# A mixture-of-experts stage that gathers its rows by a map of places instead of scattering them

## What is computed

```
gate_logits = jnp.einsum('bsd,de->bse', x, Wg)
topw, sel = jax.lax.top_k(gate_logits, K)                       # K = 3 of E = 12
topw = jax.nn.softmax(topw.astype(jnp.float32), axis=-1).astype(x.dtype)
cw = jnp.einsum('bsk,bske->bse', topw, jax.nn.one_hot(sel, E, dtype=x.dtype))
h = jax.nn.gelu(jnp.einsum('bsd,edh->ebsh', x, Wup) + bup[:, None, None, :], approximate=False)
y = jnp.einsum('ebsh,ehd->ebsd', h, Wdown) + bdown[:, None, None, :]
return jnp.einsum('bse,ebsd->bsd', cw, y)
...
x = x + jnp.tanh(g_ffn[1]) * _L1_ffn_ref(_layernorm(x, axis=-1), L1_ffn_Wg, ...)
```

## Time and profile before

| | us |
|---|---|
| runs of the kernel, median of 3 | 1554.07 |
| the three runs | 1558.92, 1545.75, 1554.07 |
| the profiled execution | 1544.64 |
| its span, first to last instruction | 1542.9 |

### The profile page before, as it was taken

How to read it: one execution, slowest core, us unless ns; L and a number is a source line. 1 busy time by engine, 2 the same in 40 slices (tenths; PEclk the granted TensorE clock), 3 DMA queues, 4 the chain that set the end, 5 groups by cost and what they waited for, 6 DMA issues and landing times. The chain is left out here.

```text
span 1542.9 us, 35004 instructions
## 1 busy us (share of the span) xinstructions
PE 1288.3 (83%) x13602; PEld 1014.9 (66%) x13602; DVE 1185.3 (77%) x2169; ACT 832.8 (54%) x1807; POOL 252.3 (16%) x213
## 2 busy tenths in 40 slices
PE   3399999668898898898957999984229999999997
PEld 2266776446676676676744676753119998989896
DVE  2656777579999999999753777767319999999995
ACT  1256676335565565565533767641117666667673
POOL 2000000000000000000000000001733454545443
PEclk7558788689999999999786999985559999999999
DMA  7000000032524523523410006200647787888771
GB/s 216 11 5 8 5 5 1 1 81 66 138 61 107 135 64 94 142 71 94 118 56 15 6 9 192 68 1 24 254 142 240 227 245 227 250 225 248 224 217 28
DMA packets 196938, 166.70 MB, mean 108 GB/s; under 512 B 72317, under 2 KB 179985, under 8 KB 196801
## 3 DMA queue, kind: packets, MB, share of 16 engines
q1 hardware_dynamic: 177856, 146.67, 31.8%
q0 software_dynamic: 12880, 13.72, 4.1%
q10 hardware_dynamic: 6064, 4.46, 1.0%
HBM read 116.78 MB, written 50.91 MB: 109 GB/s over the span
## 5 line engine op out<-in xcount | busy, mean ns | idle before, releaser
L1782 POOL DMA_INDIRECT out<-m_yo,m_meta x70 | 170.6, 2437 | 229.2 <-DVE m_yo L1900 200.0
L1804 ACT ACTIVATE m_hf<-m_ps,m_bue 128x256 f32<-128x256 f32 x280 | 117.3, 471 | 118.7 <-PE m_ps L84 117.3
L1051 ACT ACTIVATE f_pr<-f_ps,f_nb 128x256 f32<-128x256 f32 x256 | 107.4, 473 | 104.4 <-DVE f_nb L1314 98.9
L82 PE MATMUL m_ps<-m_xt,m_us 128*128 128x256 f16 x560 | 153.2, 274 | 0.0
L83 PE MATMUL m_ps<-m_xt,m_us 128*128 128x256 f16 x560 | 153.1, 273 | 0.0
L84 PE MATMUL m_ps<-m_xt,m_us 128*128 128x256 f16 x560 | 153.1, 273 | 0.0
L82 PE MATMUL m_ps<-m_ds,m_hs 128*128 128x256 f16 x560 | 152.6, 273 | 0.3 <-DVE m_yo L1900 0.3
L83 PE MATMUL m_ps<-m_ds,m_hs 128*128 128x256 f16 x560 | 152.6, 273 | 0.0
L84 PE MATMUL m_ps<-m_ds,m_hs 128*128 128x256 f16 x560 | 152.6, 273 | 0.0
L472 ACT ACTIVATE x_pr<-x_ps,x_mx 128x120 f32<-128x120 f32 x512 | 143.2, 375 | 7.8 <-DVE x_mx L686 7.8
L690 DVE SCALAR_TENSOR_TENSOR x_pt<-x_ps,x_pt 120x512 f16<-120x512 f32 x128 | 88.3, 690 | 73.2 <-ACT x_pt L480 72.5
(11 more groups left out here) (350 smaller groups left out, 3795.5 us busy)
## 6 DMA issues: line engine op xcount, KB each, us to landing
m_uraw<-in_L_ffn_Wup SPq DMA_DIRECT2D x35, 1024.0 KB
m_draw<-in_L_ffn_Wdown SPq DMA_DIRECT2D x35, 1024.0 KB
expert_in<-x_zeros SPq DMA_DIRECT2D x1, 9520.0 KB, 31.2
m_xg<-expert_in SPq DMA_DIRECT2D x35, 256.0 KB, 4.3
head_values<-f_v_row SPq DMA_DIRECT2D x16, 520.0 KB, 5.2
f_vh<-head_values SPq DMA_DIRECT2D x16, 520.0 KB, 3.6
head_outputs<-f_at_row SPq DMA_DIRECT2D x16, 512.0 KB, 2.9
f_at_in_t<-head_outputs SPq DMA_DIRECT2D x16, 512.0 KB, 6.0
```

Source lines behind the costliest of these rows:

```text
L82: pe.matmul(out, lhs[0], rhs[0], start=(n == 0), stop=False)
L1051: ins = act.activation(pr[h % 2][:, ti, :], S(h)[:, ti, :], ACT.Exp, bias=nb[h % 2][:, ti:ti + 1])
L1782: pool.indirect_dma_start(rows_of, bass.IndirectOffsetOnAxis(meta[j % RING][:, ti, 0:1].bitcast(I32), 0), yo[j % 2][:, ti, :], None, bound ...
L1804: ins = act.activation(hf[:, q, m, :], U(q)[:, m, :], ACT.Gelu, bias=weights.bue[par][:, 2 * q + m:2 * q + m + 1], scale=UNSPLIT)
```

## The change

Nothing is scattered to slots any more. `expert_in` shrinks to a table of one zero row and the 2,048 token rows in their own order: SyncE writes row 0 in attention 1 and rows 1 to 2,048 from `xn` in one plain transfer as soon as the weights are there. What has to be known now is which token row stands in each slot, the inverse of `slot_of`. It is made by matmuls: for each of the 48 groups of 128 choices VectorE writes two one-hot matrices in f16, `lane_hot` (128x128, one where the slot's place in its 128 is the column) and `column_hot` (128x70, the token's row number where the slot's group of 128 is the column; it lies in the buffer of the second block's down weights), and TensorE sums the 48 products into `MAP` (128x70). VectorE copies `MAP` to `row_of`. An empty slot has the sum 0, the zero row; a zero row has weight 0. Each block then gathers its 256 rows with two indirect transfers that POOL issues (`gather_rows`), into a ring of six buffers that also carry the token number and the weights. The first three blocks' gathers are issued in `route`; in `run_experts` POOL issues those of block j+3 ahead of the two accumulating writes of block j. Moved besides: in `route` the adds of the base output and the matmuls that feed them come after the map, one split of up weights comes ahead of the adds, and the other two splits that VectorE made there go to `run_experts`. TensorE's slots are all written out, since the ring of six does not fit a loop of two.

The diff, cut to its core:

```
@@ attention 1, SyncE
-                sp.dma_start(s.rows_in.rearrange("(n p) d -> p n d", p=P), bcast_mid(zeros[:], NB * TPB)).then_inc(rows_zeroed, 16)
+                sp.dma_start(s.rows_in[0:1, :], zeros[0:1, :]).then_inc(rows_zeroed, 16)
@@ new helper
+def gather_rows(pool, j, sem, xg, rows_in, row_of):
+    for ti in range(TPB):
+        column = j * TPB + ti
+        pool.indirect_dma_start(xg[j % RING][:, ti, :], None, rows_in[:, :],
+                                bass.IndirectOffsetOnAxis(row_of[:, column:column + 1], 0)).then_inc(sem(f"x_loaded{j % RING}"), 16)
@@ route, POOL
-            pool.wait_ge(slots_ready, 1)
-            pool.wait_ge(cw_ready, 1)
-            for n in range(CHOICES):
-                pool.indirect_dma_start(rows_in[:, :], bass.IndirectOffsetOnAxis(slot_of[:, n:n + 1], 0),
-                                        xn[:, n % TILES, :], None).then_inc(sent, 16)
-            pool.wait_ge(sent, 16 * CHOICES)
+            pool.wait_ge(table_written, 16)
+            pool.wait_ge(map_done, 1)
+            for j in range(AHEAD):
+                gather_rows(pool, j, sem, xg, rows_in, row_of)
@@ route, SyncE
+            sp.wait_ge(cw_ready, 1)
+            sp.dma_start(rows_in[1:1 + TOKENS, :].rearrange("(t p) d -> p t d", p=P), xn[:]).then_inc(table_written, 16)
             sp.wait_ge(experts_ready, 1)
@@ route, TensorE (between the transposes of cw and the matmuls with bdown)
+            for n in range(CHOICES):
+                if n % HOT_GROUP == 0:
+                    pe.wait_ge(hot_ready, n // HOT_GROUP + 1)
+                last = pe.matmul(MAP, lane_hot[:, n, :], column_hot[:, n, :], start=(n == 0), stop=(n == CHOICES - 1))
+            last.then_inc(map_ready, 1)
@@ route, VectorE
+            for n in range(CHOICES):
+                dve.tensor_scalar(lane_hot[:, n, :], lanes[:], lane_f[:, n:n + 1], None, ALU.is_equal)
+                ins = dve.tensor_scalar(column_hot[:, n, :], lanes[:, 0:COLUMNS], column_f[:, n:n + 1],
+                                        row_f[:, n % TILES:n % TILES + 1], ALU.is_equal, ALU.mult)
+                if n % HOT_GROUP == HOT_GROUP - 1:
+                    ins.then_inc(hot_ready, 1)
+            dve.wait_ge(map_ready, 1)
+            dve.tensor_copy(row_of[:], MAP).then_inc(map_done, 1)
             dve.wait_ge(experts_ready, 1)
-
+            weights.split_up_lo(dve, 0, 0)
             for tile in range(TILES):
                 dve.wait_ge(b_ready, tile + 1)
-                dve.tensor_tensor(s.x[:, tile, :], s.x[:, tile, :], ps[:, 2 + tile % 2, 0:D], ALU.add).then_inc(b_done, 1)
-            dve.wait_ge(b_done, TILES)
-            weights.split_up_lo(dve, 0, 0)
-            weights.split_up_lo(dve, 1, 1)
-            weights.split_down_lo(dve, 0, 0)
+                dve.tensor_tensor(s.x[:, tile, :], s.x[:, tile, :], BASE(tile), ALU.add).then_inc(b_done, 1)
@@ run_experts, POOL
         for j in range(NB):
+            if j + AHEAD < NB:
+                gather_rows(pool, j + AHEAD, sem, xg, rows_in, row_of)
             pool.wait_ge(y_done, TPB * (j + 2))
@@ run_experts, VectorE
         rows_part(0, 0, 0)
         rows_part(1, 1, 0)
+        up_part(1, 1, 0)
         hidden(0, 0, 0)
+        down_part(0, 0, 0)
```

More of the change, by code:

```diff
@@ L1450, in moe_stage @@
             us, dsp = two("us", [P, 2, C, HID], F16), two("ds", [P, 2, M, D], F16)
-            xg = two("xg", [P, TPB, D])
+            xg = [buf(f"xg{i}", [P, TPB, WIDE]) for i in range(RING)]
             xt = two("xt", [P, 2, C, BT], F16)
@@ L1556, in _ @@
             chain(pool.memset(before[:], 1.0))
+            chain(pool.iota(row_i[:], [[P, TILES]], base=1, channel_multiplier=1))
+            chain(pool.iota(lanes_i[:], [[1, P]], base=0, channel_multiplier=0))
+            pool.tensor_copy(row_f[:], row_i[:])
+            chain(pool.tensor_copy(lanes[:], lanes_i[:]))
             pool.iota(nth[:], [[1, NB]], base=0, channel_multiplier=0)
@@ L1726, in run_experts @@
     yo = two("yo", [P, TPB, D])
-    meta = [sb(f"meta{i}", [P, TPB, META]) for i in range(RING)]
-    x_loaded, y_added = ([sem(f"{n}{i}") for i in range(2)] for n in ("x_loaded", "y_added"))
-    meta_loaded = [sem(f"meta_loaded{i}") for i in range(RING)]
+    x_loaded = [sem(f"x_loaded{i}") for i in range(RING)]
+    y_added = [sem(f"y_added{i}") for i in range(2)]
     out_based = sem("out_based")
@@ L1752, in _ @@
         load_down = lambda j, par, turn: weights.load_down(sp, j, par)
-        def load_rows(j):
-            rows = rows_in[j * BT:(j + 1) * BT, :].rearrange("(t p) d -> p t d", p=P)
-            if j >= 2:
-                sp.wait_ge(turned, 2 + j - 1)
-            sp.dma_start(xg[j % 2][:], rows[:, :, 0:D]).then_inc(x_loaded[j % 2], 16)
-            if j >= RING:
-                sp.wait_ge(y_added[j % 2], 32 * ((j - RING) // 2 + 1))
-            sp.dma_start(meta[j % RING][:], rows[:, :, D:D + META]).then_inc(meta_loaded[j % RING], 16)
-        for j in range(3):
-            load_rows(j)
         load_up(2, 0, 1)
@@ L1862, in slot @@
             down(j, par, turn)
-        run_blocks(pe, slot)
+        for j in range(NB):
+            slot(j, j % 2, j // 2)
     @block.vector
@@ L1899, in output @@
                 dve.wait_ge(y_ready, TPB * (j + 2) + ti + 1)
[L1900 removed]
+                dve.tensor_scalar(yo[j % 2][:, ti, :], Y(ti), xg[j % RING][:, ti, bass.ds(e + D + 1, 1)], UNSPLIT,
                                   ALU.mult, ALU.mult).then_inc(y_done, 1)
```

69 lines of the change are left out of this document (43 added, 26 removed).

## The result

| | kernel before | changed kernel |
|---|---|---|
| median, us | 1547.3 (20 runs) | 1532.4 (20 runs) |
| ratio, with 95% interval | 1 | 0.988 (0.985 to 0.991) |
| profiled execution: span | 1542.9 | 1535.3 |

The changed kernel is faster by 1.2% by the ratio (it compares means and leaves out one disturbed run of 1542.76 us, and in the later job of a2_after one run of 2579.6 us of the kernel before) and by 14.9 us, 1.0%, by the medians. The forecast was a gain of 21.5 us. The predicted 1532.5 us is met to 0.1 us, but that closeness is luck: the gain was forecast 6.6 us too large, and it was taken off a median 6.8 us too high. The three runs of before that were shown are three of the twenty, whose median is 1547.3. The 14.9 us lie just under the 15.5 that the prediction took for the least that can be told from no change, but the interval of the ratio leaves no change out.

The account below looks back on a forecast made before the run. TensorE bounds the expert loop; before it, VectorE's routing chain, POOL's 48 scatters and the hand-over. 22.3 us won ahead of the loop less 0.8 in it, 21.5 off the shown median 1554.07, gave 1532.5 us, range 1519 to 1549.

Parts of the forecast that it names:

- (a): Routing stage, VectorE: four more small operations ahead of the one-hots add 0.7 us.
- (b): Routing stage, VectorE: 48 pairs of one-hot operations take 20.7 us, bounds 18.2 and 25.6.
- (c): Routing stage: the last group's eight map matmuls and the copy of the map take 1.6 us.
- (d): Routing stage, VectorE behind the map: expert register and copy take 1.5 us, the up-weight split 2.3.
- (e): Routing stage: sixteen base output adds, paced by TensorE's f32 matmuls, now come after the map and take 12.6 us.
- (f): End of routing stage: SyncE's 2,048 KB base output store takes 8.3 us to land and ends last.
- (g): Start of expert loop: joint end of stage and first transpose take 1.0 us; TensorE begins 22.3 us earlier.
- (h): First loop blocks, VectorE: two splits of 2.3 us moved there cost 0.8 us, bounds 0 and 2.3.
- It lands in an idle stretch of the DMA engines: Expert loop: a block's gathers land while DMA engines idle, within the 4.5 us allowed, so nothing was booked.
- the first rival: Expert loop: gathers land late, each block waits 0.8 or 2.5 us, giving 1558 or 1610 us; chance 0.12.
- VectorE is held by POOL: Expert loop: each gather holds VectorE for 0.83 us, +30 us over 33 blocks, giving 1562 us; chance 0.05.
- The hand-over of POOL: End of routing stage: POOL's 5.9 us in series with the store, about 1547 us; chance 0.11 shared with slow one-hots.

Follow-up runs that it names:

- a2_after: The changed kernel run again unedited, for a second profile: 1526.3 us, ratio 0.988 to the kernel before.
- e3_nowait: Changed kernel without SyncE's wait for the base output store's landing at the end of the routing stage: 1520.2 us, ratio 0.984 to the kernel before.
- e10_f32lanes: Changed kernel with the one-hots' constant row of lane numbers in f32 instead of f16: expert stage 484.6 us against 482.4.
- e11_zero: Changed kernel with the old 9,520 KB zero write put back, into a spare table nothing reads: 1530.6 us, ratio 0.989 to the kernel before.
- e5_splits: Changed kernel with the two moved weight splits put back at the end of the routing stage: 1523.7 us, ratio 0.985 to the kernel before.
- e1_ahead4: Changed kernel with gathers issued four blocks ahead instead of three: 1520.9 us, ratio 0.983 to the kernel before.
- e9_half: Changed kernel with the loop's weight loads, from block 2 on, carrying half their bytes: expert stage 476.9 us against 482.4.
- e4_interleave: Changed kernel with the sixteen base adds and their matmuls put between the one-hot pairs: 1527.6 us, ratio 0.989 to the kernel before.
- e8_all: Changed kernel with gathers four blocks ahead, no SyncE store wait, paired base tiles, four gathers in the routing stage: 1505.4 us, ratio 0.974 to the kernel before.
- e12_all_again: The e8_all version run again beside the changed kernel on one chip: 1508.2 us, ratio 0.977 to the kernel before.

## Why the prediction was right, and where its steps were not

Counted from the start of the expert stage (the prediction's times less 1043.4):

| step | predicted | measured |
|---|---|---|
| (a) one-hots begin | 33.0 | 32.9 |
| (b) one-hots end | 53.7 | 50.8 |
| (c) map copied | 55.3 | 51.8 |
| (d) split ends | 59.1 | 55.0 |
| (e) sixteen adds end | 71.7 | 68.4 |
| (f) store landed | 80.0 | 76.0 |
| (g) first transpose | 81.0 | 77.0 |

**Ahead of the loop** the mechanism was right in every step, the last included: the hidden store ends last (e3_nowait). The gain was 26.3 us against 22.3. The term that was mis-sized is (b), 17.9 us against 20.7: I had taken the f32 rate for an f16 source, and e10_f32lanes shows that the source type was it (20.4 us). The other terms come to 1.2 us less in sum: (c) and (d) 0.6 less each, (e) 0.8 more (13.4 against 12.6), (f) 0.7 less (7.6 against 8.3), (a) 0.1 less. The hand-over of 5.9 us behind the 48 scatters was read as landing and joint end together. The trace divides it otherwise: POOL's `DRAIN` starts only when the scatters have landed and lasts 3.97 us by itself (from 1139.8, line 1527).

**The zero write** was worth nothing, as booked, and the cover was the one named: a TensorE without a gap (e11_zero).

**(h), the moved splits:** 0.8 predicted, 0.7 measured (e5_splits).

**The loop** is where the sum fails: 0.8 us booked, 9.2 measured. Four parts of it, each a column of the table:

- 6.1 us are gathers that land late. The failing step is the sentence "It lands in an idle stretch of the DMA engines" and the price of 2.62 us from a SyncE load beside idle engines. The prediction's own times spoke against it: its second gather ends at 1255.65, and the idle stretch that it cites ends at 1256; in the kernel before, the share is 1.10 from 1258.5 to 1259. The reserve was sized rightly (4.5 us), and the 2.93 us issue inside VectorE's split was forecast (2.95). But the split holds POOL until the next weight load has been issued, and the transfer then shares the engines with it. At block 6 the landing takes 5.05 us from the end of the issue at 1187.42 and exceeds the reserve by a little; over the loop a second gather takes 4.3 us from there (median, 2.5 to 5.6). This is the first rival in miniature: 6.1 / 31 = 0.2 us a block, far below the 0.7 from which it would have overtaken the gain. e1_ahead4 removes it, e9_half most of it.
- 0.7 us are the splits (0.8 was booked for them, so this part was forecast).
- 1.0 us lies between the first and the third block. It is in the changed kernel twice, but not in e1_ahead4, e4_interleave or e9_half, whose instructions on TensorE there are the same. What differs is when TensorE's clock rises from 0.50 to 1.00 behind its idle time. Over the thirteen profiles the distance follows that moment, half a microsecond for each microsecond of delay: 14.8 us where it rises 5.3 us behind the first transpose (e4_interleave, e9_half), 15.0 at 5.7 (before), 15.5 at 6.6 (e8_all), 16.0 at 7.7 (changed), 16.5 at 8.7 (e10_f32lanes). Why it rises when it does, no run shows. In the changed kernel the row below, from 2.2 us behind the first transpose on, holds 22 matmuls at 0.50; in e1_ahead4 a stretch that begins 4.7 us behind it already holds 45 at 0.92.

```profile
1132.00:1137.00 5.00, 4.58 (x22) 3.50 (x23) 3.04 (x4) 2.72 (x4) 0.03 (x1) 0.50 0.59 237
```

```profile
1127.00:1132.00 5.00, 5.00 (x45) 4.32 (x43) 4.88 (x8) 3.43 (x7) 0.00 (x0) 0.92 0.29 61
```

- 1.4 us lie behind the last scatter. POOL's last scatter starts 1542.9 - 1536.38 = 6.5 us ahead of the end before and 1535.3 - 1527.32 = 8.0 after (a row of each). It is 7.8 to 7.9 in all the changed kernels but e8_all, where it is 6.1 both times. Where it lies the trace shows: the scatter lands 2.7 us behind its start in e1_ahead4 and in e8_all alike, and then POOL's `DRAIN` takes 3.39 us before, 4.79 in the changed kernel, 4.62 in e1_ahead4 and 2.99 in e8_all (below: before, changed, e8_all). Why its length differs, no run isolates; it stays open.

```profile
1536.38 1.55 POOL L1782 DMA_INDIRECT out<-m_yo,m_meta  x1 [0.30 <-issue]
L1446 POOLq DRAIN  x1: 3391/3391/3391, 1539.3 to 1539.3; - x1
```

```profile
1527.32 1.55 POOL L1811 DMA_INDIRECT out<-m_yo,m_xg  x1 [0.30 <-issue]
L1450 POOLq DRAIN  x1: 4786/4786/4786, 1530.2 to 1530.2; - x1
```

```profile
L1450 POOLq DRAIN  x1: 2989/2989/2989, 1504.9 to 1504.9; - x1
```

**The rivals.** "VectorE is held by POOL" did not happen: with POOL's gather beside it the split still takes 2.29 us (the row at 1184.27; all seventy splits of the changed kernel lie between 2.28 and 2.32), and it is POOL that grows from 0.95 to 2.93. This agrees with the rule of the Trainium skill ("SBUF — State Buffer", "SBUF: two separate sides") that the engine that starts first keeps the shared ports; a VectorE that waits for a POOL instruction that began first shows in no row read here. The hand-over of POOL did not eat the gain, since it lay under the store, but e4_interleave shows it one step below the surface.

**The sum** was -21.5; the stage gives -17.1 (499.5 to 482.4), the medians -14.9. The gain ahead of the loop was put 4.0 us too low and the loss in it 8.4 too low, so half of the error cancels. The other 4.4 us, and the 2.2 between the stage's marks and the medians, were made up by the median that was shown, 6.8 us too high. Neither was foreseen.

## What to carry to other kernels

When a transfer is moved from a queue that runs ahead (SyncE) to an engine whose instructions wait for another engine (POOL behind VectorE's splits), price its landing from the end of its issue with the loads that will then be under way, and give it a whole period of reserve more if the buffers allow; here that was one constant and 6 us. When a stage becomes short, look for the hidden work that now ends last, and then for the one behind it: the store was first, POOL's end of stage second, and removing only the first one or moving only its inputs gave 7 us or 1. Compare marks inside a stage rather than spans when what stands ahead of it varies by ten microseconds.

## What the runs showed of the hardware

- Where a stage ends with indirect gathers that POOL itself does not wait for, POOL's `DRAIN` ended 0.2 to 0.3 us behind the landing of the last one (e8_all, e4_interleave), and the next stage began 0.9 us behind that. Where POOL had seen its scatters land first, `DRAIN` took 3.0 to 4.8 us all the same (3.97 behind the 48 scatters of the kernel before, 3.39, 4.79 and 2.99 at the end of before, changed and e8_all).
- An indirect gather of 128 rows is issued in 0.94 us on a free POOL, and in 2.93 when it starts just behind the start of a VectorE split of 2.29.
- An f16 TENSOR_SCALAR costs 33 ns less than with an f32 source at 128 columns (235 against 268), 13 ns less at 70 columns with two scalars (288 against 301).
- After 9 us of idle time TensorE's clock was still at 0.50 of full speed, and it rose 5.5 us behind the first transpose in one execution (e1_ahead4) and 7.7 in another (the changed kernel); that alone makes 1 us. In e12_all_again it fell to 0.50 for a time right behind an idle stretch of 2.1 us, in e8_all behind one of 1.6 it did not; that makes 1.7 us.
